# Gathers of the last two token chunks issued later, and contexts of the second attention loaded later

## The reference, cut to what matters

```python
# first mixture: best 4 of 16 experts, weighted by a softmax of their logits
fused = sum(w[..., None] * selected_expert_outputs, axis=2)
x = x + fused
# second attention
q = layernorm(x)
logits = where(mask == 0, NEG, q @ ctx.T / 16)
a = softmax(logits) @ ctx
x = x + layernorm(a) * gamma + beta
```

## Time and profile before

| | us |
|---|---|
| median of three runs | 764.39 |
| lowest, highest | 757.75, 767.33 |
| span of the profiled execution | 778.8 |

### The profile page before, as it was taken

The page is one execution under the profiler, slowest core; times in us unless marked ns, Lnnn a source line. Parts: engine busy times, 40 slices in busy tenths (PEclk is TensorE's granted clock), DMA queues, the critical chain, the costliest instruction groups (busy, mean ns, idle before and its releaser), DMA issues.

```text
span 778.8 us, 15559 instructions
## 1 busy us (share of the span) xinstructions
PE 705.9 (91%) x5728; PEld 572.2 (73%) x5728; DVE 537.9 (69%) x1189; ACT 414.7 (53%) x786; POOL 431.0 (55%) x451
## 2 busy tenths in 40 slices
PE   5799999999998866999999999996989779889987
PEld 2577777778776766899999999973464446657677
DVE  4688778778787474047777777716555978887576
ACT  3565665665654331366666666531338956664332
POOL 4648644645644117467778888544022859984130
PEclk9999999999999877899999999998999999999999
DMA  8201101101020396879989999987523500001000
GB/s 333 98 2 56 56 1 54 54 0 54 0 109 2 130 406 274 314 260 409 371 331 341 344 333 336 365 332 273 218 77 112 227 0 1 1 0 42 1 0 28
DMA packets 20476, 123.50 MB, mean 159 GB/s; under 512 B 2288, under 2 KB 6784, under 8 KB 13120
## 3 DMA queue, kind: packets, MB, share of 16 engines
q1 hardware_dynamic: 17488, 114.72, 38.8%
q0 software_dynamic: 2928, 8.00, 2.8%
HBM read 111.90 MB, written 10.81 MB: 158 GB/s over the span
## 4 chain that ended last, share of the span: by engine, by line
PE 73%; DVE 10%; ACT 6%; issue 4%; POOL 3%; another core or an unknown queue 1%; DMA 1%; SPq 0%; DVEq 0%; ACTq 0%; PEldq 0%
PE banks L2049 63%; PE banks L2118 7%; POOL inject L985 1%; DMA ctx_raw<-in_ctxT 1%; ACT probs L1049 1%; DVE negmax_raw L1503 1%; DVE banks L1930 1%; PE banks L2563 1%; DVE shown L1919 1%; ACT banks L1291 1%; PE banks L2286 1%; ACT ctx_hi L1035 1%; DVE X L2008 1%; DVE shown L1940 0%
## 5 line engine op out<-in xcount | busy, mean ns | idle before, releaser
L2049 PE MATMUL banks<-xT,raw 128*128 128x128 f32 x992 | 152.3, 277 | 0.6 <-DVE xT L1718 0.6
L2049 PEld LDWEIGHTS banks<-xT,raw 128*128 128x128 f32 x992 | 135.7, 193 | 3.3 <-issue 1.2
L918 POOL TENSOR_TENSOR w_lo<-raw,w_hi 128x1024 fp32r<-128x1024 f32 x50 | 118.0, 2387 | 1.7 <-ACT w_hi L1142 1.0
L1173 ACT ACTIVATE banks<-banks,later 128x128 f32<-128x128 f32 x200 | 67.9, 340 | 56.2 <-PE banks L2049 55.0
L985 POOL TENSOR_TENSOR inject<-BCbc,drive 128x1024 f32<-128x1024 f32 x32 | 74.9, 2358 | 20.2 <-DVE drive L1877 9.5
L1078 ACT ACTIVATE probsT<-banks 128x512 f32<-128x512 f32 x64 | 38.3, 598 | 85.2 <-PE banks L2118 85.0
L1724 DVE CAST mid_hi<-banks 128x128 fp32r<-128x128 f32 x200 | 57.8, 289 | 33.6 <-ACT banks L1173 31.9
L1503 DVE TENSOR_REDUCE negmax_raw<-banks 128x1 f32<-128x1024 f32 x64 | 77.5, 1211 | 2.8 <-PE banks L2049 2.8
L1049 ACT ACTIVATE probs<-banks,negmax 128x1024 f32<-128x1024 f32 x64 | 71.2, 1113 | 10.9 <-DVE negmax L1505 10.7
L2118 PE MATMUL banks<-table,probs 128*128 128x128 f32 x512 | 71.0, 283 | 2.1 <-DVE probsT L1476 2.1
L2049 PE MATMUL banks<-w_hi,mid_hi 128*128 128x256 f32 x200 | 72.6, 363 | 0.0
(11 more groups left out here) (344 smaller groups left out, 1787.9 us busy)
## 6 DMA issues: line engine op xcount, KB each, us to landing
raw<-in_w SPq DMA_DIRECT2D x31, 2048.0 KB, 8.4
ctx_raw<-in_ctxT SPq DMA_DIRECT2D x8, 1024.0 KB, 4.8
ctxT<-in_ctxT SPq DMA_DIRECT2D x4, 2048.0 KB, 10.5
ctxN<-in_ctxN SPq DMA_DIRECT2D x4, 2048.0 KB, 11.0
x_slots<-zero SPq DMA_DIRECT2D x1, 3968.0 KB, 12.1
y_slots<-y_tile POOLq DMA_DIRECT2D x29, 128.0 KB, 7.1
wf<-in_w SPq DMA_DIRECT2D x9, 384.0 KB, 5.3
BCbc<-bc_rows SPq DMA_DIRECT2D x6, 512.0 KB, 7.3
```

What stands on the lines that cost most here:

```text
L918: nc.gpsimd.tensor_tensor(w2_lo[i % WB][:, cols], raw[i % WB][:, EW // 2:][:, cols], w2_hi[i % 2][:, cols].bitcast(F32), ALU.subtract).the ...
L1173: nc.scalar.activation(to, held, ACT.Gelu, bias=b1[:, bass.ds(at + u, 1)]).then_inc(gelu_done, 1)
L2049: return nc.tensor.matmul(o, lhsT, rhs, start=start, stop=stop)
```

## The change: what it does

- SP: T(0) and N(0) stay. T(1) keeps its place in the loop, but first waits until the store of tile 28 has landed. T(2) and N(1), in this order, are issued behind the loop and behind a wait for the gathers of chunk 1. N(2), T(3) and N(3) keep their conditions.
- GpSimd: the gathers of chunks 0 and 1 stay. Then it waits for the copy of the last expert tile, computes the 1/sqrt of chunks 0 and 1, issues the gathers of chunk 2, computes the 1/sqrt of chunk 2, and issues the gathers of chunk 3.
- VectorE: combine 2 moves behind arrive 1 and greatest 0, combine 3 behind greatest 1; the statistics of chunk 1 move ahead of arrive 0.

```diff
                 if i == TILES - WB:
                     masks(range(2, TC))
-                if i >= TILES - WB:
-                    p, normal = divmod(i - (TILES - WB), 2)
-                    (context_N if normal else context_T)(p)
-
+                if i == TILES - WB:
+                    context_T(0)
+                if i == TILES - WB + 1:
+                    context_N(0)
+                if i == COLD - 1:
+                    sp.wait_ge(y_stored[i % YB], 16 * (i // YB + 1))
+                    context_T(1)
+
+            sp.wait_ge(gathered[1], 16 * TOP0)
+            context_T(2)
+            context_N(1)
             for k in range(YB):
                 sp.wait_ge(y_stored[k], y_stores(k))
             sp.wait_ge(bias_done, len(SUM_BANKS))
...
             gather_rows(0)
             gather_rows(1)
+            pool.wait_ge(last_taken, last_before + LAST)
+            rstd_of(4, 0)
+            rstd_of(4, 1)
             gather_rows(2)
-            rstd_of(4, 0)
-            gather_rows(3, range(TOP0 // 2))
-            rstd_of(4, 1)
-            gather_rows(3, range(TOP0 // 2, TOP0))
             rstd_of(4, 2)
+            gather_rows(3)
             rstd_of(4, 3)
...
             norm_begin(4, 0)
             add_sums(1, TC)
+            norm_begin(4, 1)
             arrive(0)
-            norm_begin(4, 1)
+            arrive(1)
+            greatest(0)
             combine(2)
-            arrive(1)
             norm_begin(4, 2)
-            greatest(0)
+            greatest(1)
             arrive(2)
             combine(TC - 1)
             dve.sem_inc(x_updated, 1)
             norm_begin(4, 3)
-            greatest(1)
             arrive(3)
```

More of the change, by code:

```diff
@@ L933, in store_tile, with gather_rows @@
                 pool.dma_start(y_slots[i * P:(i + 1) * P, :], y_tile[i % YB][:]).then_inc(y_stored[i % YB], 16)
-            def gather_rows(t, places=range(TOP0)):
-                for j in places:
+            def gather_rows(t):
+                for j in range(TOP0):
                     k = TOP0 * t + j
```

## The result

The changed kernel took 771.41 us, median of 17 runs (765.53 to 774.56); the kernel before, beside it on the same chip, 764.14 us, median of 17 (757.75 to 768.59). The ratio is 1.0098, 95% interval 1.0077 to 1.012: about 1% slower, inside the 2% that count as no change. The forecast was 770.4 us.

The account below looks back on a forecast made before the run. TensorE, busy for 91% of the span, was taken as the bound, through when score2(3) starts. Terms: 2.5 + 4.8 - 1.3 = 6.0 us slower, 764.4 + 6.0 = 770.4 us; 80% range 758 to 779.

Parts of the forecast that it names:

- add_sums 8.3 us earlier than in the profile: End of the expert tiles: without TensorE's stall, add_sums starts at 526.0 instead of 534.36 us.
- Chunk 2 lands 6.0 us after its last issue: Chunk 2's moved gathers, under three context loads, land 6.0 us after the last issue, bounds 1.5 and 8.
- The rival in which the gathers get their turn (761 us): Chunk 2's gathers land 1.5 us after their last issue despite the loads: not slower, 761 us; chance 0.23.
- T(3) issued 26.7 us after add_sums: SP issues load T(3) only after combine 3, at 552.7 us, with add_sums at 526.0; today it goes out at 549.05.
- score2(3) waits for its context: TensorE, ready at 555, stands 5 us ahead of score2(3) until T(3) lands at 560.0 us.
- Slower by more through new stalls beside the gathers (780 us): Rival: gathers beside score2(0), score2(2) and mix2(0) stall TensorE, and chunk 2 lands at 8 us: 780 us; chance 0.10.
- longer series, less what score2(3) had in hand: From add_sums to score2(3): 9.3 us for chunks 2 and 3 in series, less 1.3, gives +8.0 us.
- lower clock in score2(3): After TensorE's wait score2(3) runs at a lower clock: 1.5 us added, bounds 0 and 3.6.
- The 1.3 us that the forecast took off: In the kernel before, chunks 2 and 3's gathers meet T(2) and N(2): 1.3 us of its lead lost, between 0 and 2.
- then add_sums starts today where combine 1 ends, 525.37 + 4.16 = 529.5: In the kernel before without the stall, add_sums starts at 529.5 us, so 4.8 of the 8.3 us are no gain.
- I take it that timed runs do not have the stall: TensorE's three unexplained gaps, 15.7 us, belong to the profiled execution; timed runs have little or none, their median 14.4 us lower.
- stall in the timed runs: Rival: timed runs have TensorE's stall and the change removes it, 8.3 us won, 10.8 lost: 767 us; chance 0.22.

Follow-up runs that it names:

- e7: The changed kernel with N(1), and N(2) behind it, issued only when chunk 2 has landed; ratio 1.0096 to the kernel before.
- e6: The changed kernel without the wait for the last tile's copy, chunk 2's gathers straight behind chunk 1's; ratio 1.0147 to the kernel before.
- e8: The kernel before with the SP and VectorE parts of the change, without GpSimd's; ratio 0.9998 to the kernel before.
- e11: The kernel before with only T(2) and N(1) held behind the gathers of chunk 1; ratio 1.0026 to the kernel before.
- e1: The kernel before, unedited, profiled a second time; ratio 0.9976, profiled span 760.8 us.
- after: The changed kernel with the whole change, as profiled for the main comparison; 771.41 us, ratio 1.0098 to the kernel before.
- first profile: The kernel before, unedited, in the profiled execution that the prediction read; span 778.8 us.
- e9: The kernel before with SP's part, and also N(1) behind chunk 3's landing and N(2) behind T(3); ratio 1.0008 to the kernel before.
- e12: The changed kernel again, unedited, on the third chip; ratio 1.0094 to the kernel before.
- e2: The kernel before with only SP's part of the change; ratio 0.9927 to the kernel before.
- e3: The kernel before with only GpSimd's part of the change; ratio 1.0108 to the kernel before.
- e5: The changed kernel with chunk 3's gathers straight behind chunk 2's, ahead of chunk 2's 1/sqrt; ratio 1.005 to the kernel before.
- e4: The kernel before with only VectorE's part of the change; ratio 1.0023 to the kernel before.

## Why the prediction was right, and where it was not

**The time and the mechanism were right.** Point by point, from the turn of the gates where two kernels are compared:

- First gather 2.3 us earlier: it was 3.0 (8.0 to 5.0 us after the gates).
- add_sums 8.3 us earlier than in the profile: 8.7 (27.8 to 19.1).
- Chunk 2 lands 6.0 us after its last issue: 6.07 (521.46 to 527.53). e7 shows that the loads are the cause: 1.75 with N(1) and N(2) held back. The rival in which the gathers get their turn (761 us) fell with that. By the Trainium skill, DMA: Bandwidth & Descriptors, Queues, rings and completion order, each DMA engine takes turns between queues by the packet. The prediction named this as the condition of that rival, in which chunk 2 lands near the unloaded value; the measured 6.07 us, in a stretch at 413 GB/s, against 1.75 without the load, doesn't bear that out, and the runs don't show why.
- Chunk 3 lands in 1.5 us without a load: 1.83.
- T(3) issued 26.7 us after add_sums: 27.2. On the chip 7.3 us: 7.61 by the chain.
- score2(3) waits for its context: 3.43 us, plus 5.55 ahead of chunk 2's turn; I had put 5 us at one place.
- Slower by more through new stalls beside the gathers (780 us): the changed kernel's gathers have none beside them. The rival fell for this kernel. A stall beside gathers is real on the two slower chips, but beside twelve in a row (e6, e8 to e11), not beside groups of four.

**All three terms of the sum were mis-sized, and it was luck that they cancelled.** The right comparison is with e1, the kernel before without the stall:

| step | forecast, against the timed kernel | measured, after against e1 |
|---|---|---|
| add_sums earlier | -3.5 | -6.9 (26.0 to 19.1) |
| longer series, less what score2(3) had in hand | +8.0 | +9.9 (T(3) 13.9 later after add_sums; 4.0 of slack used) |
| lower clock in score2(3) | +1.5 | +3.0 |
| sum | +6.0 | +6.1 |

The forecast's rows: -3.5 is 8.3 less 4.8, and +8.0 is 9.3 less 1.3. The slack: in e1 score2(3) starts 11.66 us after T(3) is issued (530.53 to 542.19), in the changed kernel 7.65 (539.99 to 547.64). The 1.3 us that the forecast took off, for the loads that the kernel before would meet itself, is not seen: e1 issues T(3) 13.3 us after add_sums, the first profile 14.7. The clock: score2(3) takes 6.64 us instead of 3.65, and in the profile eight matmuls of the next stage take 3.63 instead of 2.01, as the chain of e1 has them:

```profile
542.19 3.65 PE banks L2049 x16
...
565.53 2.01 PE banks L2049 x8
```

The second 1.6 us is not shown to come of the change. The first profile has it too, without a wait for T(3):

```profile
582.35 3.30 PE banks L2049 x8
```

and so do e9 (3.07) and e11 (3.13), while e7 and e12, which wait for T(3), take 2.01. So it is left out of the table. The measured sum of 6.1 stands beside 7.3 us between the medians. Between the two ends counted from the gates (278.1 and 269.5) it is 8.6 us: 6.1, these 1.6, and about 1 us that is not traced.

**The step that failed: "then add_sums starts today where combine 1 ends, 525.37 + 4.16 = 529.5".** It took chunk 1's landing of at most 3.0 us from an execution in which the stall had kept T(2) away. Without the stall T(2) collides with chunk 1, and the landing is 5.91 us. The forecast had add_sums 4.8 us earlier in a kernel before without the stall; e1 has it 1.8 us earlier (27.8 to 26.0). I had allowed this collision for chunks 2 and 3, not for chunk 1. So the later loads are worth twice what I gave them, as e2 shows (0.73% when nothing spends it).

**"I take it that timed runs do not have the stall"** was right on the chip of the comparison and wrong as a general statement. I took the stall for something of the profiled execution, as its three gaps sum to 15.7 us and the execution was 14.4 us above the median. That match is in part luck. Of the 18.0 us between the two profiles of the kernel before, 15.3 lie before the turn of the gates, where the two gaps beside the scatters have 7.48; the third gap, of 8.22 us, is worth 1.5 us at score2(3) (52.4 against 50.9). The profiles of e6 and e8 to e11, with twelve gathers in a row, have the last tile copied 21.7 to 23.1 us after the gates, and the kernel before is 9 us slower on those chips in its timed runs. It has no trace there; by the other kernels' traces the time is lost mostly beside the scatters, ahead of the gates, and that the kernel before loses them there too is an inference. The changed kernel has little of it (copy at 18.4 in e12), and add_sums starts at 20.1 us there, 5 to 6 us ahead of those. It doesn't pay: with T(3) 27.8 us behind add_sums the kernel is 0.94% slower there too, where the rival "stall in the timed runs" (767 us) asks for 0.3%.

**Where the 1% comes from**, then: GpSimd's part. e3 has it alone (1.0108), e8 takes it out (0.9998), e5 takes out the half that lies in chunk 3's place (1.005), and e7 shows that the loads only choose which chunk waits. The gathers of the last two chunks were hidden behind the first layer norms; behind the copy of the last tile and in series with the 1/sqrt they are on the path to T(3), whose memory the last combine frees (with VectorE's old order, in e3, on the path to greatest 1). What SP's part wins at add_sums is spent twice over.

**Open:** what makes TensorE stand still beside long runs of indirect DMAs on some chips, and whether SP's part alone, 0.73% faster on the first chip, wins anything on a chip with the stall; e2 wasn't run there, and e8 and e9, which have SP's part with other edits, came out at 0.9998 and 1.0008.

## What to carry to other kernels

Before a move of DMA work, follow what its completion frees: here the last gather frees the memory of the last load, and 14 us of delay there cost more than 7 us won at the front. Read a wait's length together with what was in flight beside it; a stall elsewhere in the same execution may have kept a colliding transfer away. Delaying loads so that small gathers pass first is worth trying by itself, without reordering the gathers: here it gained 0.73% on one chip, and variants of it nothing clear on the two others. And before a difference between two profiles is put down to a gap, count where it arises: a mark that comes at the same place in the work, such as the turn of the gates here, splits it.

## What the runs showed of the hardware

- Four gathers (512 KB) land 1.8 to 2.0 us after their last issue with no load beside them (after, e2, e3, e6, e7, e12), 5.3 to 7.0 us under context loads (after, e1 to e5, e7, e12), and once in between, 4.8 us, under the end of a load (chunk 3 of the first profile). Issuing one takes mostly 1.26 us from start to start, in every run.
- TensorE can fall behind, or stand still, beside long runs of indirect DMAs with no wait that the program has. With twelve gathers in a row its last tile was copied 17.4 us after the gates on the first chip and 21.7 to 23.1 us on the two others; with eight in a row, 17.9 to 18.4 us there. Beside 16 scatters it ran 207 to 223 matmuls in 30 us on the first chip (after, e1 to e4) and 130 to 149 on the two others (e5 to e12). The number of gathers goes with it on those chips; the resource behind it isn't shown.
- After TensorE had stood for 5.55 us the granted clock was 0.50 (531.2 to 536.0 us), the lower level of 1.2 GHz, and after 3.43 us more ahead of score2(3) it was 0.54 on average over its matmuls, which took 6.64 instead of 3.65 us. Here a wait of TensorE was paid twice.
